# An LSTM with an adapter on one core: projection by quadrants, weights in another order, the second block projected ahead

## The reference

```
x = x + lstm(x, h0=cond)                 # step t: z = x_t @ Wx + b + h @ Wh, split into i, f, o, g (256 each)
                                         # c = sig(f)*c + sig(i)*tanh(g);  h = sig(o)*tanh(c)
x = x + adapter(x, cond)                 # c = layernorm(cond)*gamma + beta; w = gelu(c @ W1 + bias1) @ W2 + bias2
                                         # w gives a1, b1, a2, b2 (rank 8) for each sequence
                                         # mid = gelu(x @ base_down + (x @ a2) @ b2^T)
                                         # out = mid @ base_up^T + (mid @ b1) @ a1^T
```

## Time and profile before

| | us |
|---|---|
| median of 3 runs | 608.72 (607.85 to 609.86) |
| profiled execution | 610.4 |
| its span, first to last instruction | 608.4 |
| PE busy in the span | 589.4 (97%) |
| DVE busy | 476.1 (78%) |
| ACT busy | 375.6 (62%) |
| POOL busy | 49.6 (8%) |

### The profile page before, as it was taken

One profiled execution on the slowest core, in us unless ns is written; L12 is line 12 of the kernel. 1 busy time (PEld: TensorE's weight loads), 2 busy tenths in 40 slices (PEclk: granted clock), 3 DMA queues, 4 the chain that ended last, 5 costly groups with the idle time before them and its releaser, 6 DMA issues.

```text
span 608.4 us, 33942 instructions
## 1 busy us (share of the span) xinstructions
PE 589.4 (97%) x14092; PEld 437.7 (72%) x14092; DVE 476.1 (78%) x2549; ACT 375.6 (62%) x2154; POOL 49.6 (8%) x96
## 2 busy tenths in 40 slices
PE   8697999999999999999999999999999999999997
PEld 5564667777777777777777777777777777777886
DVE  2576787888888888888888888888888888888773
ACT  1364566666666666666666666666666666666663
POOL 5001320000000000000000000000000000000000
PEclk9799899999999999999999999999999999999999
DMA  7889340232322123333212233321223333123301
GB/s 193 218 222 307 62 59 13 38 56 56 56 56 39 39 37 56 55 56 56 42 38 34 56 56 55 55 48 34 34 54 56 56 55 53 32 31 46 56 20 29
DMA packets 32139, 39.73 MB, mean 65 GB/s; under 512 B 3905, under 2 KB 29809, under 8 KB 30962
## 3 DMA queue, kind: packets, MB, share of 16 engines
q1 hardware_dynamic: 31282, 36.51, 30.7%
q0 software_dynamic: 704, 1.05, 1.1%
HBM read 16.05 MB, written 4.19 MB: 33 GB/s over the span
## 4 chain that ended last, share of the span: by engine, by line
PE 95%; issue 1%; DMA 1%; POOL 1%; DVE 1%; SPq 0%; ACT 0%; POOLq 0%; ACTq 0%
PE z L676 36%; PE x_bank L480 19%; PE z_o L676 9%; PE aux L506 8%; PE out_bank L530 7%; PE aux L491 3%; PE aux L458 3%; PE out_bank L562 2%; PE aux L513 2%; PE out_bank L605 2%; DMA seed<-proj 1%; PE out_bank L551 1%; PE x_bank L551 1%; PE x_bank L506 0%; DMA x_nat<-in_x 0%
## 5 line engine op out<-in xcount | busy, mean ns | idle before, releaser
L676 PE MATMUL z<-wh,h_t 128*16 128x96 f32 x8160 | 237.2, 249 | 3.7 <-issue 3.3
L676 PEld LDWEIGHTS z<-wh,h_t 128*16 128x16 f32 x8160 | 152.8, 96 | 112.4 <-DVE h_t L849 80.4
L829 DVE STREAM_TRANSPOSE z<-z 128x96 f32<-128x96 f32 x512 | 152.6, 298 | 73.9 <-PE z L676 50.0
L401 ACT ACTIVATE gates<-z 128x48 f32<-128x48 f32 x512 | 107.6, 210 | 123.2 <-DVE z L829 123.0
L480 PE MATMUL x_bank<-wx,x_t 128*128 128x256 f32 x512 | 156.6, 394 | 0.5 <-ACT x_t L333 0.5
L339 ACT ACTIVATE z<-seed 128x96 f32<-128x96 f32 x512 | 127.5, 249 | 5.8 <-DMA seed<-proj 5.8
L676 PE MATMUL z_o<-wh,h_t 128*16 128x64 f32 x4080 | 104.9, 219 | 0.3 <-issue 0.3
L839 DVE SCALAR_TENSOR_TENSOR prod<-gates 128x32 f32<-128x32 f32 x512 | 98.1, 192 | 0.0
L343 ACT ACTIVATE z_o<-seed 128x64 f32<-128x64 f32 x256 | 58.3, 228 | 60.3 <-DVE h_t L849 60.3
L844 DVE SCALAR_TENSOR_TENSOR gates<-prod 128x16 f32<-128x16 f32 x512 | 84.6, 165 | 8.7
L480 PEld LDWEIGHTS x_bank<-wx,x_t 128*128 128x128 f32 x512 | 81.3, 197 | 6.0 <-issue 1.7
(11 more groups left out here) (123 smaller groups left out, 441.7 us busy)
## 6 DMA issues: line engine op xcount, KB each, us to landing
seed<-proj SPq DMA_DIRECT2D x128, 128.0 KB, 4.3
w<-in_L_cond_W SPq DMA_DIRECT2D x4, 2048.0 KB, 10.7
x_nat<-in_x SPq DMA_DIRECT2D x32, 128.0 KB, 4.3
out<-y_nat SPq DMA_DIRECT2D x32, 128.0 KB, 4.3
wx<-in_L_cond_Wx SPq DMA_DIRECT2D x2, 512.0 KB, 5.5
wh<-in_L_cond_Wh SPq DMA_DIRECT2D x2, 256.0 KB, 6.9
wh<-in_L_cond_Wh SPq DMA_DIRECT2D x1, 512.0 KB, 5.9
w_bias<-in_L_cond_bias POOLq DMA_DIRECT2D x4, 128.0 KB, 6.0
```

Of the source, the lines that this page charges most:

```text
L401: act.activation(gates[s % 2][m][:, 0:3 * B].rearrange("p (g b) -> p g b", b=B), zt[m].rearrange("p (g c) -> p g c", c=C)[:, :, 0:B], ACT. ...
L676: ins = pe.matmul(dst, h_prev[:, kc, :], rhs, start=False, stop=(kc == 1), skip_group_check=True)
L829: dve.transpose(zt[m], z_bank[m][:, 0:GC]).then_inc(turned[m], 1)
```

## The change

The constants `rows_of` hold 2 or 4 in their first row and zeros elsewhere, and `b_pad` holds b in its first row and zeros elsewhere, so that the bias matmuls use all 128 rows of the array and give the scaled bias in the quadrants' order; `b_all` is then a plain copy. A quarter of the projection is now a quadrant with all its gates, ordered half by half and within a half as i, f, g, o (the order that `wx` now has too), read from `wx` in runs of 32 columns; `proj` is written contiguously, and each quadrant's seed transfer waits for its own quarter only. In `seed`, a half has its 96 columns for a z bank and 32 for z_o behind them. The g columns of Wx and Wh are loaded first and doubled first. cond and b are issued by ACT. Block 1 is projected whole in front of the steps. bias2 is loaded behind step 0.

```diff
-WARM_UP = 4
+WARM_UP = 6
@@ tiles
-        ones = sb("ones", [P, P])
+        rows_of = {n: sb(f"row_{n}", [P, P]) for n in (2, 4)}
-        b_row = sb("b_row", [1, G * H])
+        b_pad = sb("b_pad", [P, G * H])
@@ SP load_seed
-                sp.wait_ge(xz_ready, f.k * XQ + XQ)
                 for j in range(NQ):
+                    sp.wait_ge(xz_ready, f.k * XQ + (j + 1))
                     sp.dma_start(seed[f.par][32 * j:32 * j + B, :, :], proj[f.par][:, ZW * j:ZW * (j + 1)])
@@ SP start
-            sp.dma_start(b_row[:, :], b.rearrange("(a n) -> a n", a=1)).then_inc(w_loaded["b"], 16)
+            load_cols(wx, Wx, 2 * H, 3 * H, H, "wx_g")
             load_cols(wx, Wx, 0, 0, 2 * H, "wx_if")
-            load_cols(wx, Wx, 2 * H, 2 * H, 2 * H, "wx_og")
-            sp.dma_start(c_in[:, :], cond).then_inc(w_loaded["cond"], 16)
-            load_cols(wh, Wh, 2 * H, 3 * H, H, "wh")
-            load_cols(wh, Wh, 0, 0, 2 * H, "wh")
-            load_cols(wh, Wh, 3 * H, 2 * H, H, "wh")
+            load_cols(wx, Wx, 3 * H, 2 * H, H, "wx_o")
+            load_cols(wh, Wh, 2 * H, 3 * H, H, "wh_g")
+            load_cols(wh, Wh, 0, 0, 2 * H, "wh_if")
+            load_cols(wh, Wh, 3 * H, 2 * H, H, "wh_o")
@@ ACT
+            act.dma_start(c_in[:, :], cond).then_inc(w_loaded["cond"], 16)
+            act.wait_ge(b_zeroed, 1)
+            act.dma_start(b_pad[0:1, :], b.rearrange("(a n) -> a n", a=1)).then_inc(w_loaded["b"], 16)
             act.wait_ge(zeroed, 1)
             act.activation(gelu_0[:, :], zeros[0:1, 0:1], ACT.Gelu)
...
-                act.activation(z_bank[m][:, 0:GC], seed[buf][:, s, GC * m:GC * (m + 1)], ACT.Copy)\
+                act.activation(z_bank[m][:, 0:GC], seed[buf][:, s, P * m:P * m + GC], ACT.Copy)\
...
-                act.activation(o_bank[:, 0:OC], seed[buf][:, s, NM * GC:ZW], ACT.Copy).then_inc(seeded_o, 1)
+                act.activation(o_bank[:, 0:OC].rearrange("p (m c) -> p m c", c=C),
+                               seed[buf][:, s, :].rearrange("p (m q) -> p m q", m=NM)[:, :, GC:P], ACT.Copy)\
...
             evacuate_x(Blk(0, 0))
-            act.wait_ge(w_loaded["wx_og"], 16)
-            double_g(wx, 3 * H, wx_ready)
+            act.wait_ge(w_loaded["wx_g"], 16)
+            double_g(wx, wx_ready)
+            act.wait_ge(w_loaded["wh_g"], 16)
+            double_g(wh, wh_ready)
             evacuate_x(Blk(0, 1))
-            act.wait_ge(w_loaded["wh"], 48)
-            double_g(wh, 2 * H, wh_ready)
@@ PE project, first block's waits and the operands
+                    if i == 0 and not f.at_least(1):
+                        pe.wait_ge(wx_ready, 1)
+                        pe.wait_ge(w_loaded["wx_if"], 16)
+                        pe.wait_ge(w_loaded["wx_o"], 16)
+                    if i == 2 and not f.at_least(1):
+                        pe.wait_ge(ht_ready[1], 1)
...
-                    ins = pe.matmul(x_bank[q % 2][:, 0:XW], x_t[f.k % N_X][:, kc, :], wx[:, kc, q * XW:(q + 1) * XW],
+                    ins = pe.matmul(x_bank[q % 2][:, 0:XW].rearrange("p (m g c) -> p m g c", m=NM, c=C),
+                                    x_t[f.k % N_X][:, kc, :],
+                                    wx[:, kc, :].rearrange("p (g m j c) -> p j m g c", g=G, m=NM, c=C)[:, q],
@@ PE start
             transpose_x(Blk(0, 0), both)
-            pe.wait_ge(w_loaded["b"], 16)
-            for i, bank in enumerate((out_bank, x_bank[1])):
-                pe.matmul(bank[:, :], ones[0:1, :], b_row[0:1, i * 2 * H:(i + 1) * 2 * H],
-                          start=True, stop=True).then_inc(b_psum, 1)
-            project(Blk(0, 0), range(N_PIECES))
             pe.wait_ge(w_loaded["cond"], 16)
             for m in both:
-                ins = pe.transpose(out_bank[:, m * B:(m + 1) * B], c_in[:, m * P:(m + 1) * P], ident[0:B, 0:B])
+                ins = pe.transpose(x_bank[1][:, m * B:(m + 1) * B], c_in[:, m * P:(m + 1) * P], ident[0:B, 0:B])
             ins.then_inc(h0_psum, 1)
+            pe.wait_ge(rows_made, 2)
+            pe.wait_ge(w_loaded["b"], 16)
+            for i, bank in enumerate((out_bank, tanc_bank)):
+                for place, gate in enumerate((0, 1, 3, 2)):
+                    quarters = bank[:, :].rearrange("p (j m g c) -> p g j m c", j=2, m=NM, c=C)
+                    ins = pe.matmul(quarters[:, place], rows_of[4 if gate == 3 else 2][:, :],
+                                    b_pad[:, gate * H:(gate + 1) * H]
+                                    .rearrange("p (m j c) -> p j m c", m=NM, c=C)[:, 2 * i:2 * i + 2],
+                                    start=(place == 0), stop=True, skip_group_check=True)
+                ins.then_inc(b_psum, 1)
+            project(Blk(0, 0), range(N_PIECES))
             transpose_x(Blk(0, 1), both)
-            project(Blk(0, 1), range(N_PIECES // 2))
+            project(Blk(0, 1), range(N_PIECES))
+            pe.wait_ge(w_loaded["wh_if"], 16)
+            pe.wait_ge(w_loaded["wh_o"], 16)
@@ PE behind steps 0 and 1
-                            if s < 2:
-                                project(Blk(0, 1), range(4 + 2 * s, 6 + 2 * s))
@@ DVE
-                dve.tensor_tensor(gate_cols(proj[f.par], q), x_bank[q % 2][:, 0:XW].rearrange(units, m=NM, c=C),
-                                  b_all[:, q * XW:(q + 1) * XW].rearrange(units, m=NM, c=C), ALU.add)\
+                dve.tensor_tensor(proj[f.par][:, q * XW:(q + 1) * XW], x_bank[q % 2][:, 0:XW],
+                                  b_all[:, q * XW:(q + 1) * XW], ALU.add).then_inc(xz_ready, 1)
...
             dve.memset(zeros[:, :], 0.0).then_inc(zeroed, 1)
+            dve.memset(b_pad[:, :], 0.0).then_inc(b_zeroed, 1)
+            for row in rows_of.values():
+                dve.memset(row[:, :], 0.0).then_inc(rows_zeroed, 1)
...
+            for n, row in rows_of.items():
+                dve.memset(row[0:1, :], float(n)).then_inc(rows_made, 1)
...
+            for i, bank in enumerate((out_bank, tanc_bank)):
+                dve.wait_ge(b_psum, i + 1)
+                dve.tensor_copy(b_all[:, i * 2 * H:(i + 1) * 2 * H], bank[:, :]).then_inc(b_ready, 1)
@@ POOL
-            pool.memset(ones[:, :], 1.0).then_inc(consts_made, 1)
...
+            pool.wait_ge(ht_ready[1], 2)
             bias_q = bias2.rearrange("(q j n) -> j q n", q=4, j=NQ)
             for j in range(NQ):
                 pool.dma_start(w_bias[32 * j:32 * j + B, :, :], bias_q[j].partition_broadcast(B))\
```

More of the change, by code:

```diff
@@ L139, in lstm_adapter @@
         consts_made = sem("consts_made")
+        b_zeroed, rows_zeroed, rows_made = sem("b_zeroed"), sem("rows_zeroed"), sem("rows_made")
         zeroed = sem("zeroed")
         w_loaded = {n: sem(f"{n}_loaded") for n in
-                    ("wx_if", "wx_og", "wh", "b", "down", "up", "ln", "cond", "w1")}
+                    ("wx_g", "wx_if", "wx_o", "wh_g", "wh_if", "wh_o", "b", "down", "up", "ln", "cond", "w1")}
         w2_loaded = [sem(f"w2_loaded{q}") for q in range(4)]
@@ L182, in lstm_adapter @@
         block = ctx.enter_context(nc.Block())
[L184 to L190, removed]
         class Blk:
@@ L375, in make_weights, with double_g @@
                                    ACT.Copy).then_inc(wt_ready, 1)
-            def double_g(t, lo, ready):
-                act.activation(t[:, :, lo:lo + H], t[:, :, lo:lo + H], ACT.Copy, scale=2.0).then_inc(ready, 1)
+            def double_g(t, ready):
+                act.activation(t[:, :, 2 * H:3 * H], t[:, :, 2 * H:3 * H], ACT.Copy, scale=2.0).then_inc(ready, 1)
             evacuate_x(Blk(0, 0))
-            act.wait_ge(w_loaded["wx_og"], 16)
-            double_g(wx, 3 * H, wx_ready)
+            act.wait_ge(w_loaded["wx_g"], 16)
+            double_g(wx, wx_ready)
+            act.wait_ge(w_loaded["wh_g"], 16)
+            double_g(wh, wh_ready)
             evacuate_x(Blk(0, 1))
-            act.wait_ge(w_loaded["wh"], 48)
-            double_g(wh, 2 * H, wh_ready)
             act.wait_ge(bits_set, 1)
@@ L790, in _ @@
             dve.memset(zeros[:, :], 0.0).then_inc(zeroed, 1)
+            dve.memset(b_pad[:, :], 0.0).then_inc(b_zeroed, 1)
+            for row in rows_of.values():
+                dve.memset(row[:, :], 0.0).then_inc(rows_zeroed, 1)
             for m in both:
                 dve.memset(gates[0][m][:, 3 * B:4 * B], 0.0).then_inc(zeroed, 1)
[L794 to L806 removed]
+            dve.wait_ge(rows_zeroed, 2)
+            for n, row in rows_of.items():
+                dve.memset(row[0:1, :], float(n)).then_inc(rows_made, 1)
             dve.wait_ge(w_loaded["cond"], 16)
@@ L820, in _ @@
             dve.tensor_scalar(c_stat[:, 3:4], c_stat[:, 2:3], 1.0 / D, LN_EPS, ALU.mult, ALU.add).then_inc(ln_step, 1)
-            for q in range(2):
+            dve.wait_ge(h0_psum, 1)
+            for m in both:
+                dve.tensor_scalar(h_first[:, m, :], x_bank[1][:, m * B:(m + 1) * B], 2.0, None, ALU.mult)\
+                   .then_inc(ht_ready[m], 1)
+            for i, bank in enumerate((out_bank, tanc_bank)):
```

(17 more changed lines are left out.)

26 lines of the change are left out of this document (2 added, 24 removed).

## The result

The changed kernel takes 610.97 us (median of 20 runs, 610.03 to 613.28), the kernel before 609.70 (20 runs, 607.85 to 611.52): ratio 1.0024, 95% interval 1.0015 to 1.0033. The forecast was 602.4, and faster; it is 0.24% slower. The profiled execution took 610.63 us, against 610.4 before. The start became nearly as much shorter as forecast, and within eight steps all of it was lost again.

A forecast was written before the change was run, and what follows sets the result against it. TensorE, holding 95% of the last chain, was taken as the bound. An earlier start (4.1 us) plus shorter steps 0 and 1 (2.2) made 6.3 us off, from median 608.72 to 602.4; range 600.8 to 604, chance 0.55.

The forecast's parts named there:

- T: Time at which block 0's projection ends on TensorE: 12.5 us forecast, 14.13 before.
- S: Time of step 0's first gate matmul: T + 5.3 = 17.8 us forecast, 4.1 us earlier than 21.87.
- steps 0 and 1: First two steps of block 0: 2.21 us each instead of 4.24 and 2.37, saving 2.2 us.
- The rival that kept the clock low: Start of block 0: slow clock or late b keeps the projection behind 10 us; 604.7 us, chance 0.17.
- The strided read: Later steps' projection, moving operand read in eight runs of 32 columns: zero cost; rival at half rate 735 us, chance 0.03.
- What costs nothing: Moved loads and issues, including bias2 behind step 0: free, since users come later (bias2's some 17 us, W2 15 us cover).
- stalls of blocks 0 and 1 shift: Unexplained TensorE waits by W2 loads: one more, 2.8 us, 605.2, chance 0.10; one or both gone, 599.6 or 596.9, together 0.10.

The follow-up runs named there:

- no_bias2: The changed kernel without the four bias2 loads, bias2 left out of the computation: 607.79 us, ratio 0.9962 to the kernel before.
- warm4: The changed kernel with four warm-up matmuls instead of six, eight TensorE instructions fewer ahead of the steps: 610.91 us, ratio 1.0024 to the kernel before.
- light: The changed kernel without bias2, block 1's seeds and base_down ahead of the first W2 load, second W2 load held until step 6 is seeded: 604.14 us.
- seed1_first: The changed kernel with block 1's seeds and base_down issued ahead of the first W2 load: 607.79 us, ratio 0.9976 to the kernel before.

## Why the prediction was wrong

**The start (T, S, steps 0 and 1): right.** b landed at 5.04 (5.4 forecast), 2.93 after its issue. The Wx transfer that SP issued at 2.10, next to b's 2.11, landed at 6.37: ACT's transfer was not behind SP's, as the rule of the Trainium skill that the prediction cites has it. The bias ended at 8.93 (7.5 to 8.8), at the slow rate (3.76 us for its 16 instructions); three evacuations follow the first by 0.78, 0.87 and 0.86 (0.86). T was 13.03 instead of 12.5, the last seed issue 0.47 behind it (0.5), its landing 4.21 (4.3), the first gate matmul at 18.20 (17.8), under a granted clock of 1.00. The rival that kept the clock low fell with this. Steps 0 and 1 took 2.09 and 2.21 (2.21). At step 2 the sum was 5.98 of 6.3. The median that the forecast started from, 608.72 of three runs, was 1.0 below that of twenty; this is a part of the distance from 602.4, and not a matter of the mechanism.

**The strided read at nothing: right.** 442.28 for 200 steps against 442.16 in the earlier trace rows.

**"What costs nothing": this step failed.** The bias2 loads were put down as free because their user was 17 us away, and W2's as covered because it had 15 us. Both covers held: in the kernel after TensorE and VectorE wait nowhere for W2 or bias2. The price was another user of the same DMA engines, the fetch of TensorE's code: a stall of 7.36 us, 3.0 of them by bias2 (`no_bias2`), and about 1.4 of low clock behind it. The step counted for each moved transfer who waits for it, and not what else passes while it does. It also left out transfers that the change moves without an edit: block 1 is projected earlier, so its seeds, base_down and the second W2 load are issued 12 us earlier. (A rival did say that the W2 loads start earlier against the steps.)

**The rival "stalls of blocks 0 and 1 shift": the right mechanism, the wrong size and chance.** It had one more stall at 2.8 us, from an average over block 1, and 0.10; measured were 7.36 and some 1.4 of clock. It called the two waits of the earlier trace rows unexplained and gave them half of block 1's excess each, 2.8, where they took 1.3 and 1.9. Their place in the middle of a run of matmuls, the busy DMA engines ahead of them (85% from 47.6 to 51.5, and q1 alone at 91% from 54 to 58.4, without a code packet in either) and the code packet shortly before TensorE goes on were in the trace of before and could have told what they are, and then that a change that packs transfers together ahead of step 5 can lengthen them.

**Where the gain went.** Shown: the place of the stall is set by an instruction count (`warm4`, and the 72 waits); its length falls with most loads taken away or moved from the 10 us ahead of it (7.4; 4.4 without bias2; 4.0 with W2 in pieces; 2.9 with the seeds first; 1.3 in `light`), but not with the second W2 load held (7.4); with the loads away most of the gain is there (`light`, ratio 0.9917). The traces also show that the packet was late. Taken in order, the 112 packets match the blocks of 256 that begin at instruction 450, 706 and so on. From the 21st packet on, in all 19 traces, a packet starts 0.8 us (median, at most 2.7) after TensorE begins the block before its own; the packet of the stall started 9.6 after that in the kernel after, 6.8 in `no_bias2`, 5.5 in `seed1_first` and 3.7 in `light`. Not shown: why a code packet waits so long. The Trainium skill ("DMA: Bandwidth & Descriptors", Queues, rings and completion order) has each DMA engine go round between queues packet by packet. By that rule a code packet would wait for about one packet of each other queue. Here some 1,200 others went in between, on 16 engines, if a packet of the profile is one of that rule. When the packet was asked for is not in the trace, so that it stood in line all that time is likely from the 0.8 us elsewhere, and not shown. Nor is it settled how much of the wait goes by bytes and how much by the number of packets.

## What to carry to other kernels

In this fully unrolled kernel the code is a stream that goes over the same DMA engines as the data; in the first microseconds, when many loads are queued, TensorE can stop in the middle of a run of matmuls for want of code, and the profile then shows "issue", idle engines everywhere and full DMA queues, a multiple of 256 instructions apart. Before a load is moved to where its own user has slack, look for such stops in the trace of before, look at what will be in flight when the next block of code is due, and prefer parts over one long load, and one copy over sixteen. A start that is made faster brings every later transfer forward against the steps, the ones that the diff does not touch too.

## What the runs showed of the hardware

- TensorE's code passed in 112 packets of 16.4 KB, one for 256 instructions. All 72 of TensorE's unexplained waits (over 0.25 us, in 19 traces) stand 193 to 195 over a multiple of 256 in its count of instructions, and end 2.2 to 3.8 us after a code packet starts.
- The granted clock was still 0.99 from 32 to 34, with TensorE idle since 29.92 in the kernel after, and 0.50 from 34 to 36; in `light` a stall of 1.27 left it at 1.00.
- The last seed transfer (128 KB) took 4.21 us in the kernel after and 7.20 with bias2 in flight; bias2 itself 6.0 in the earlier trace rows and 13.7 in the kernel after.
- A matmul of one row on each of four row groups, 256 columns (L612), took as long as the full W2 piece beside it: 0.55 against 0.56 for eight instructions.
